# A macaron block on one core: other orders in the opening, at the handover between stages and in the last stage

## The chip, the cores and the metric

The kernel runs on one core of a Trainium2 chip. The metric is the device time of one execution in microseconds, as the median of several runs. The core has five engines with queues of their own: TensorE (PE; matrix products, transposes and weight loads), VectorE (DVE), ScalarE (ACT), GpSimd (POOL) and SyncE (SP), which here only issues transfers. Each works through its instructions strictly in the order in which they are written, and engines wait for each other through semaphores. An instruction that waits holds up everything behind it on its engine.

## The reference

The block takes x of 4 × 1024 tokens with 1024 features and adds three parts to it, one after the other. FFN is a gated linear layer, used twice with the same weights:

```
dots = softmax(LN(x) @ centroids.T / 0.1); hits = dots > 0.01
query_sel = any(hits, axis=1); cluster_sel = any(hits, axis=0)   # over all tokens
out = where(query_sel[:, None] & cluster_sel[assignments], LN(x) @ weight.T + bias, 0)

x = x + 0.5 * FFN(LN(x))
x = x + attention(LN(x))      # each token by itself: 32 heads attend to 32 heads, 8 kv heads repeated 4 times
x = x + 0.5 * FFN(LN(x))
```

`cluster_sel` needs the hits of all tokens, so no output of a FFN is final before the last token has been through its softmax.

## The kernel before, in words

The 4096 tokens are 32 tiles of 128. A matrix product is made of three matmuls for each of 8 blocks of 128 features (k-groups): operands are split into a high and a low part, and high·high, high·low and low·high are summed (`product`, which also takes a table `between` of work to put ahead of a k-group). A product of a tile has two halves of 512 columns, written (t, h) here. To split a tile, ScalarE copies the turned tile to the high part (`high_...`), VectorE subtracts to get the low part (`low_...`), and TensorE needs both.

**Stage one** (`product_first`) makes the first FFN. In the opening the weight rows come in eight loads and are turned by TensorE in 16 blocks of 4 transposes (`transpose_rows`), each into one of five banks by the table `W_BANK`; a block waits until the low part of the block that had the bank before (`low_rows`) is made. Block j covers rows of group j // 2 and half the features. Tiles 0 to 3 are turned by TensorE. From tile 4 on a normed tile is stored to memory (`store_normed`), loaded back in 32-token blocks by four loads (`load_blocks`), and turned within blocks by VectorE (`turn_first`). Tiles go in pairs: `pair_first` makes the softmax logits of two tiles, ScalarE copies them (`copy_pair`), `fold_pair` transposes them, VectorE and ScalarE make the softmax. VectorE evicts each half with the bias (`read_first`), GpSimd masks it by token (`select_tokens`), SP stores it to `f1_d` (`store_first`). All transfers of the stage stand in the one SP queue, in an order that is written by hand.

**The handover.** When the last pair is through its softmax, `select_count` and `select_rows` give the column mask on TensorE, ScalarE copies it (`select_mask`), GpSimd masks tile 0 of `f1_d` and adds x (`mask_first`, `add_first`), VectorE takes statistics, GpSimd the factors, ScalarE the norm, and TensorE transposes. **Stage two** runs over i, with several tiles in flight: products of the last tiles of stage one, q, k and v, scores, heads, and products of the second FFN. q and k of a tile go to memory and back in head order (`qkv_d`); scores wait for that.

**The last stage** runs over 14 late tiles (`LATE`, number v): `transpose_late`, `high_late`, `low_late`, two half products, and `read_late` and `add_late`, beside `finish_ready` for tiles whose product is already made. `store_late` stores a late tile.

TensorE's transposes of late tile v + 1 wait for `low_late(v)`:

```
                def transpose_late(v):
                    pe.wait_ge(yl, v)
                    ...
                        pe.wait_ge(lol, v - 1)
                    transposes(pe, late_y[v % 2]).then_inc(tl, 1)
```

## Time and profile before

| | before |
|---|---|
| median of 3 runs | 1248.04 us (1247.98 to 1249.10) |
| profiled execution, its own time | 1247.12 us |
| its span, first to last instruction | 1245.3 us |
| TensorE busy | 1214.8 us, 98% |
| VectorE busy | 855.7 us, 69% |
| ScalarE busy | 412.6 us, 33% |
| GpSimd busy | 422.6 us, 34% |
| mean granted TensorE clock | 0.993 |

Times in the trace are us from the start of the span. Where a row ends in brackets, the number is how long the engine stood idle before it, and behind the arrow is what released it. `PEclk` is the granted clock of TensorE as a share of full (2.4 GHz). The chain that ended last consists of TensorE for 87% of the span.

### The profile page before, as it was taken

The page shows a single profiled execution, that of the slowest core. Times are in us where ns is not written, and L with a number is a line of the kernel's source. Part 1 is how long each engine was busy: PE and PEld are TensorE (multiplying, and loading weights), DVE is VectorE, ACT ScalarE, POOL GpSimd, SP SyncE. Part 2 cuts the span into 40 slices and gives each one's busy share as a digit, 9 for nine tenths or more (in the row PEclk, how much of TensorE's full clock was granted, in tenths as well). Part 3 has the DMA queues.
Part 4 walks back from the last instruction along what each step waited for, and adds up shares of the span by engine and source line. Part 5 has one row for each costly group of instructions (what it writes and reads, how often), then busy time and mean ns, then how long its engine had stood idle before and what let it go on. Part 6 is the DMA issues. An engine that isn't in the chain of part 4 may idle for free.

```text
span 1245.3 us, 21665 instructions
## 1 busy us (share of the span) xinstructions
PE 1214.8 (98%) x8488; PEld 1042.0 (84%) x8488; DVE 855.7 (69%) x1270; ACT 412.6 (33%) x590; POOL 422.6 (34%) x551
## 2 busy tenths in 40 slices
PE   6999999999997999999999999999999999999998
PEld 5778888888886788888888888888888888887886
DVE  5654465456453377888888888888888875289787
ACT  4222223222220234444444444444444443212120
POOL 1225454543423634323333333333332200040332
PEclk9999999999999899999999999999999999999999
DMA  7376776786663345555555555555565555116875
GB/s 262 102 211 191 238 208 187 189 231 190 161 181 123 106 118 159 157 140 161 154 142 152 152 154 162 135 163 137 153 163 145 142 144 171 51 57 238 293 283 194
DMA packets 318694, 208.54 MB, mean 167 GB/s; under 512 B 258304, under 2 KB 281344, under 8 KB 318592
## 3 DMA queue, kind: packets, MB, share of 16 engines
q1 hardware_dynamic: 303712, 187.74, 53.1%
q10 hardware_dynamic: 14880, 19.40, 4.5%
q8 instruction: 68, 1.11, 0.4%
q14 instruction: 34, 0.28, 0.1%
HBM read 118.49 MB, written 88.60 MB: 166 GB/s over the span
## 4 chain that ended last, share of the span: by engine, by line
PE 87%; DVE 4%; DMA 4%; ACT 2%; SPq 1%; issue 1%; POOL 1%; POOLq 0%; DVEq 0%; ACTq 0%
PE ps_b L268 13%; PE ps_b L270 13%; PE ps_b L269 13%; PE ps_a L268 10%; PE ps_a L270 10%; PE ps_a L269 10%; PE ps_t L275 6%; PE ps_s L1351 5%; PE ps_s L282 2%; PE ps_s L284 2%; DMA y_scratch<-xa 2%; PE ps_s L1401 2%; SPq L402 1%; DMA ya_tok<-y_scratch 1%; DVE ya_tok L939 1%
## 5 line engine op out<-in xcount | busy, mean ns | idle before, releaser
L268 PE MATMUL ps_a<-w_hi,odd_hi 128*128 128x512 f32 x464 | 187.0, 403 | 0.0
L270 PE MATMUL ps_a<-w_hi,odd_lo 128*128 128x512 f32 x464 | 182.4, 393 | 0.0
L269 PE MATMUL ps_a<-w_lo,odd_hi 128*128 128x512 f32 x464 | 182.0, 392 | 0.0
L268 PE MATMUL ps_b<-proj_hi,y_hi 128*128 128x256 f32 (+1 forms) x512 | 177.7, 347 | 0.0
L270 PE MATMUL ps_b<-proj_hi,y_lo 128*128 128x256 f32 (+1 forms) x512 | 172.7, 337 | 0.0
L269 PE MATMUL ps_b<-proj_lo,y_hi 128*128 128x256 f32 (+1 forms) x512 | 172.0, 336 | 0.0
L301 POOL TENSOR_TENSOR var_eps<-moments,eps 128x1 f32<-128x1 f32 x96 | 18.2, 190 | 412.8 <-DVE moments L297 412.8
L665 POOL TENSOR_TENSOR x_ring<-x_ring,f_tmp 128x1024 f32<-128x1024 f32 x32 | 77.0, 2407 | 151.0 <-DVE probs L1115 117.3
L966 DVE TENSOR_TENSOR f_out<-ps_b,bias_a 128x512 f32<-128x512 f32 x30 | 20.7, 689 | 143.6 <-PE ps_b L270 143.6
L611 POOL TENSOR_SCALAR f_out<-f_out,token_on 128x1024 f32<-128x1024 f32 x30 | 85.6, 2854 | 83.2 <-DVE f_out L966 82.9
L270 PEld LDWEIGHTS ps_b<-proj_hi,y_lo 128*128 128x128 f32 x512 | 97.1, 190 | 10.8
L269 PEld LDWEIGHTS ps_b<-proj_lo,y_hi 128*128 128x128 f32 x512 | 97.3, 190 | 9.4
L268 PEld LDWEIGHTS ps_b<-proj_hi,y_hi 128*128 128x128 f32 x512 | 97.2, 190 | 9.0
L270 PEld LDWEIGHTS ps_a<-w_hi,odd_lo 128*128 128x128 f32 x464 | 87.8, 189 | 19.0
L268 PEld LDWEIGHTS ps_a<-w_hi,odd_hi 128*128 128x128 f32 x464 | 88.1, 190 | 17.6
L269 PEld LDWEIGHTS ps_a<-w_lo,odd_hi 128*128 128x128 f32 x464 | 88.2, 190 | 17.2
L310 ACT ACTIVATE q_diag<-x_ring,norms 128x1024 f32<-128x1024 f32 x64 | 79.6, 1244 | 62.2 <-PE ps_s L1351 40.4
L704 POOL TENSOR_TENSOR late<-late,mask 128x1024 f32<-128x1024 f32 x18 | 46.0, 2569 | 137.9 <-DMA late<-x_scratch 91.2
L1073 DVE TENSOR_TENSOR y_lo<-ps_t,y_hi 128x1024 fp32r<-128x1024 f32 x32 | 39.2, 1225 | 65.7 <-ACT y_hi L851 65.7
L268 PE MATMUL ps_b<-w_hi,odd_hi 128*128 128x512 f32 x208 | 81.7, 393 | 0.0
L270 PE MATMUL ps_b<-w_hi,odd_lo 128*128 128x512 f32 x208 | 81.2, 390 | 0.0
L269 PE MATMUL ps_b<-w_lo,odd_hi 128*128 128x512 f32 x208 | 81.1, 390 | 0.0
(189 smaller groups left out, 2722.5 us busy)
## 6 DMA issues: line engine op xcount, KB each, us to landing
xa<-in_L_attn_x SPq DMA_DIRECT2D x32, 512.0 KB, 5.1
f_tmp<-f_scratch SPq DMA_DIRECT2D x32, 512.0 KB, 4.6
x_ring<-in_L_attn_x SPq DMA_DIRECT2D x32, 512.0 KB, 3.3
f_scratch<-f_out SPq DMA_DIRECT2D x30, 512.0 KB, 3.8
x_scratch<-x_ring SPq DMA_DIRECT2D x30, 512.0 KB, 3.3
y_scratch<-xa SPq DMA_DIRECT2D x28, 512.0 KB, 4.5
ya_tok<-y_scratch SPq DMA_DIRECT2D x112, 128.0 KB, 3.3
late<-x_scratch SPq DMA_DIRECT2D x22, 512.0 KB, 7.2
```

Source lines behind the costliest of these rows:

```text
L268: pe.matmul(acc, hi[:, k, :], w_h[:, k, cols], start=(k == 0), stop=False)
L269: pe.matmul(acc, hi[:, k, :], w_l[:, k, cols], start=False, stop=False)
L270: last = pe.matmul(acc, lo[:, k, :], w_h[:, k, cols], start=False, stop=(k == KB - 1))
L275: last = pe.transpose(ps_t[:, k, :], src[:, k * P:(k + 1) * P], ident[:, :])
L282: last = pe.matmul(pair_ps, cen[:, k, :], hi[:, k, :, :], start=(k == 0), stop=(k == KB - 1))
L284: pe.matmul(pair_ps[0:NCL, :], cen[:, k, 0:NCL], lo[:, k, :, :], start=False, stop=False)
L310: return act.activation(y, x, ACT.Identity, bias=norms[of][:, t, 0:1], scale=norms[of][:, t, 1:2])
L611: pool.tensor_scalar(f_out[t % 2][:, :], f_out[t % 2][:, :], token_on[0][:, t:t + 1], None, ALU.mult).then_inc(f1_on, 1)
L665: pool.tensor_tensor(x_ring[t % RING][:, :], x_ring[t % RING][:, :], f_tmp[:, :], ALU.add).then_inc(x1, 1)
L704: pool.tensor_tensor(f[:, :], f[:, :], mask[:, :], ALU.mult).then_inc(s_masked, 1)
L1073: dve.tensor_tensor(y2_lo[:, :, :], ps_t[:, :, :], y2_hi[:, :, :].bitcast(F32), ALU.subtract).then_inc(lo2, 1)
L1351: last = pe.matmul(ps_s[:, j * P:(j + 1) * P], q_diag[:, j * P:(j + 1) * P], k_blocks[:, j, :, :], start=True, stop=True)
```

## The change

It makes no other arithmetic, apart from two half products that are made in two parts of 256 columns.

- Opening: the first half product (0,0) is made by `product_opening` in two parts, the first of which needs blocks 0 to 3 only; blocks go to other banks; norms, low parts and statistics stand in another order on ScalarE and VectorE.
- Tiles 4 and 5: statistics, factors and norm stand earlier; `fold_pair` and `pair_first(2)` stand later on TensorE.
- Tile 31: loaded earlier, stored directly behind tile 30 on a semaphore of its own, its low part ahead of an eviction, and the logits of its pair behind the half product instead of inside it.
- Handover: the loads for stage two (`load_attention`) stand ahead of the store of tile 28; the first transposes of stage two stand inside product (29,1); VectorE evicts (29,1) behind the first statistics.
- Last stage: `low_late(4)` one tile earlier; the last half product, its eviction and its store in two parts.

```diff
-        W_BANK = [0, 1, 2, 3, 0, 1, 2, 3, 1, 3, 4, 1, 3, 4, 1, 3]
+        W_BANK = [0, 1, 2, 3, 4, 1, 2, 3, 4, 1, 3, 4, 1, 3, 4, 1]
...
+        def late_parts(v, h):
+            if v == NL - 1 and h == 1:
+                return [slice(HALF, HALF + QUARTER), slice(HALF + QUARTER, EMB)]
+            return [half(h)]
...
                 def load_blocks(t):
-                    sp.wait_ge(y_stored, 16 * (t + 1 - BY_PE))
+                    if t == LAST:
+                        sp.wait_ge(y_last_stored, 32)
+                    else:
+                        sp.wait_ge(y_stored, 16 * (t + 1 - BY_PE))
...
+                def load_attention():
+                    sp.wait_ge(lo1, NT)
+                    sp.wait_ge(f1_stored[0], 16)
+                    sp.dma_start(f_tmp[:, :], f1_d[0]).then_inc(f_in, 16)
+                    for t in range(RING - 1):
+                        sp.dma_start(x_ring[t % RING][:, :], x_d[t]).then_inc(x_in[t % RING], 16)
...
-                    if 2 * p + 5 < NT:
+                    if 2 * p + 5 < LAST:
                         load_first(2 * p + 5)
                     if 2 * p + 4 < NT:
                         store_normed(2 * p + 4)
+                        if 2 * p + 5 == LAST:
+                            store_normed(LAST)
                         load_blocks(2 * p + 4)
                     if 2 * p + 6 < NT:
                         load_first(2 * p + 6)
+                    if p == NP - 2:
+                        load_attention()
                     store_first(2 * p)
-                    if 2 * p + 5 < NT:
+                    if 2 * p + 5 < LAST:
                         store_normed(2 * p + 5)
+                    if 2 * p + 7 == LAST:
+                        load_first(LAST)
...
@@ -635,11 +653,9 @@
-                    if 2 * p + 5 < NT and p > 0:
+                    if 2 * p + 5 < NT:
                         factors_first(2 * p + 5)
                     select_tokens(2 * p)
-                    if p == 0:
-                        factors_first(2 * p + 5)
...
@@ -746,32 +762,31 @@
                 high_rows(0)
+                norm_first(0)
                 high_rows(1)
-                norm_first(0)
                 high_rows(2)
-                high_rows(3)
                 high_first(0)
-                for j in range(4, 8):
+                for j in range(3, 8):
                     high_rows(j)
...
                     high_first(2 * p + 2)
+                    if p == 0:
+                        norm_first(2 * p + 4)
                     pair_soft_exp(act, p)
                     if p == 0:
-                        norm_first(2 * p + 4)
                         high_first(2 * p + 3)
...
@@ -973,21 +991,21 @@
-                for j in range(4):
+                for j in range(3):
                     low_rows(j)
                 low_first(0)
-                for j in range(4, 8):
+                for j in range(3, 6):
                     low_rows(j)
                 stats_first(1)
...
                 read_first(1, 0)
+                stats_first(4)
                 low_first(2)
                 pair_soft_in(dve, 0)
                 pair_soft_out(dve, 0, 0)
-                stats_first(4)
+                stats_first(5)
                 read_first(0, 1)
                 low_first(3)
-                stats_first(5)
...
                 turn_first(LAST)
+                low_first(LAST)
                 read_first(NT - 5, 1)
-                low_first(LAST)
...
+                    if i == 0:
+                        read_first(NT - 3, 1)
...
-                        if 3 < v + 1 < NL:
+                        if 4 < v + 1 < NL:
                             low_late(v + 1)
                     base_late(v)
+                    if v == 2:
+                        low_late(4)
...
@@ -1225,6 +1252,15 @@
+                def product_opening(between_a, between_b):
+                    hi, lo = first_set(0)
+                    pe.wait_ge(lo1, 1)
+                    pe.wait_ge(wt_lo, 4)
+                    product(pe, ps_a[:, 0:QUARTER], hi, lo, w_hi, w_lo, slice(0, QUARTER), between_a)
+                    pe.wait_ge(wt_lo, 8)
+                    product(pe, ps_a[:, QUARTER:HALF], hi, lo, w_hi, w_lo, slice(QUARTER, HALF),
+                            between_b).then_inc(ffn1[0], 1)
...
                 for p in range(1, NP - 2):
-                    fold_pair(p)
-                    product_first(2 * p, 0)
+                    product_first(2 * p, 0, {3 if p == 1 else 1: lambda: fold_pair(p)})
                     product_first(2 * p, 1)
-                    pair_first(p + 1)
+                    if p > 1:
+                        pair_first(p + 1)
                     product_first(2 * p + 1, 0)
+                    if p == 1:
+                        pair_first(p + 1)
...
-                product_first(NT - 4, 0, {5: lambda: pair_first(NP - 1)})
-                product_first(NT - 4, 1, {2: lambda: fold_pair(NP - 1)})
-                product_first(NT - 3, 0, {1: lambda: select_count(pe, 0), 4: lambda: select_rows(pe, 0)})
-                product_first(NT - 3, 1)
+                product_first(NT - 4, 0)
+                pair_first(NP - 1)
+                product_first(NT - 4, 1, {1: lambda: fold_pair(NP - 1)})
+                product_first(NT - 3, 0, {1: lambda: select_count(pe, 0), 3: lambda: select_rows(pe, 0)})
+                product_first(NT - 3, 1, {6: lambda: transpose_second(0)})
```

TensorE at the start of the program; `w_raw` are the weight rows, `even_hi` and `even_lo` the parts of tile 0, `ya_tok` ahead of the product tile 0 and inside it the centroids. Before:

```order
3 L275 MATMUL ps_t<-ident,ya_tok 128x128 x8
4 L1214 MATMUL ps_a<-ident,w_raw 128x128 x8
5 L1214 MATMUL ps_b<-ident,w_raw 128x128 x8
6 L268 MATMUL ps_a<-w_hi,even_hi 128x512
7 L269 MATMUL ps_a<-w_lo,even_hi 128x512
8 L270 MATMUL ps_a<-w_hi,even_lo 128x512
9 L1244 MATMUL ps_s<-ident,ya_tok 128x64 x8
```

Of the change, the same place:

```order
3 L283 MATMUL ps_t<-ident,ya_tok 128x128 x8
4 L1241 MATMUL ps_s<-ident,w_raw 128x128 x4
5 L1241 MATMUL ps_a<-ident,w_raw 128x128 x4
6 L1241 MATMUL ps_b<-ident,w_raw 128x128 x8
7 L276 MATMUL ps_a<-w_hi,even_hi 128x256
8 L277 MATMUL ps_a<-w_lo,even_hi 128x256
9 L278 MATMUL ps_a<-w_hi,even_lo 128x256
10 L1288 MATMUL ps_s<-ident,ya_tok 128x64 x8
```

The blocks ahead of the product are the same, block 4 in another bank, and the product's matmuls have 256 columns.

SP's queue at the end of stage one, from the store of tile 30 on; `ya_tok<-y_scratch` are the four loads of a tile's blocks, `f_scratch<-f_out` a `store_first`. Before:

```order
143 L391 DMA y_scratch<-xa 128x1024
144 L402 DMA ya_tok<-y_scratch 32x32x32 x4
145 L407 DMA f_scratch<-f_out 128x1024
146 L391 DMA y_scratch<-xa 128x1024
147 L402 DMA ya_tok<-y_scratch 32x32x32 x4
148 L407 DMA f_scratch<-f_out 128x1024 x2
149 L454 DMA f_tmp<-f_scratch 128x1024
150 L456 DMA x_ring<-in_L_attn_x 128x1024 x4
```

Of the change:

```order
143 L399 DMA y_scratch<-xa 128x1024 x2
144 L413 DMA ya_tok<-y_scratch 32x32x32 x4
145 L418 DMA f_scratch<-f_out 128x1024
146 L413 DMA ya_tok<-y_scratch 32x32x32 x4
147 L418 DMA f_scratch<-f_out 128x1024
148 L423 DMA f_tmp<-f_scratch 128x1024
149 L425 DMA x_ring<-in_L_attn_x 128x1024 x4
150 L418 DMA f_scratch<-f_out 128x1024
```

The stores of tiles 30 and 31 now stand together ahead of the loads of tile 30, and the five loads of stage two stand ahead of the last of these stores of `f_out`, that of tile 28.

VectorE in the last stage, from `base_late(2)` on (first row); L1164 and L1166 are the two operations of `finish_ready`, L1146 and L1153 `read_late` and `add_late`, and the `odd_lo` row is `low_late(4)`. Before:

```order
1142 L1140 SCALAR_TENSOR_TENSOR late<-k_diag,token_on,late 128x1024
1143 L1164 SCALAR_TENSOR_TENSOR x_ring<-k_diag,token_on,x_ring 128x1024
1144 L1166 SCALAR_TENSOR_TENSOR x_ring<-late,token_on,x_ring 128x1024
1145 L1164 SCALAR_TENSOR_TENSOR x_ring<-k_diag,token_on,x_ring 128x1024
1146 L1166 SCALAR_TENSOR_TENSOR x_ring<-late,token_on,x_ring 128x1024
1147 L1146 SCALAR_TENSOR_TENSOR v_diag<-ps_a,token_on,mask 128x512
1148 L1153 TENSOR_TENSOR late<-late,v_diag 128x512
1149 L1146 SCALAR_TENSOR_TENSOR v_diag<-ps_a,token_on,mask 128x512
1150 L1153 TENSOR_TENSOR late<-late,v_diag 128x512
1151 L1053 TENSOR_TENSOR odd_lo<-ps_t,odd_hi 128x8x128
```

Of the change:

```order
1145 L1159 SCALAR_TENSOR_TENSOR late<-k_diag,token_on,late 128x1024
1146 L1070 TENSOR_TENSOR odd_lo<-ps_t,odd_hi 128x8x128
1147 L1183 SCALAR_TENSOR_TENSOR x_ring<-k_diag,token_on,x_ring 128x1024
1148 L1185 SCALAR_TENSOR_TENSOR x_ring<-late,token_on,x_ring 128x1024
1149 L1183 SCALAR_TENSOR_TENSOR x_ring<-k_diag,token_on,x_ring 128x1024
1150 L1185 SCALAR_TENSOR_TENSOR x_ring<-late,token_on,x_ring 128x1024
```

The low part has moved ahead of four finishing operations and four of late tile 2.

## Rows read from the trace of the kernel before

**Rows 1.** TensorE's waits, whole span: operation, what released it, us in total, times, longest

```profile
PE ps_s L282 <- DVE odd_lo L944: 4.7, 2, 3.9
...
PE ps_s L282 <- DVE even_lo L944: 2.9, 2, 2.5
PE ps_s L289 <- ACT pair_sums L732: 2.1, 1, 2.1
PE ps_t L275 <- DVE odd_lo L1053: 1.7, 1, 1.7
```

**Rows 2.** Windows, whole trace: busy us of the engines, granted clock, DMA share, GB/s

```profile
core 0: us, PE busy (x) PEld busy (x) DVE busy (x) ACT busy (x) POOL busy (x), PEclk, DMA share, GB/s
...
16.00:20.50 4.50, 4.50 (x20) 3.46 (x20) 1.02 (x3) 1.13 (x3) 1.03 (x4) 0.62 1.02 406
...
54.50:58.50 4.00, 4.00 (x12) 3.23 (x13) 1.50 (x3) 0.25 (x1) 1.21 (x1) 0.57 1.06 259
...
378.50:382.00 3.50, 3.50 (x17) 3.50 (x18) 0.00 (x0) 0.00 (x1) 0.57 (x1) 0.55 0.37 150
...
407.30:413.00 5.70, 5.70 (x18) 4.83 (x19) 1.23 (x1) 1.01 (x1) 5.56 (x3) 0.50 0.24 95
...
431.00:1100.00 669.00, 668.95 (x5890) 587.68 (x5890) 517.01 (x742) 276.49 (x422) 202.12 (x309) 1.00 0.52 143
```

**Rows 3.** Timeline of TensorE in the opening: start, us, what, idle before

```profile
15.77 0.47 PE L268 MATMUL ps_a<-w_hi,even_hi 128*128 128x512 f32 x1 [3.10 <-DVE w_lo L950]
...
70.00 0.38 PE L282 MATMUL ps_s<-even_hi,cen 128*128 128x256 f32 x1 [2.55 <-DVE even_lo L944]
...
94.03 0.28 PE L282 MATMUL ps_s<-odd_hi,cen 128*128 128x256 f32 x1
```

**Rows 4.** Timeline of VectorE in the opening

```profile
13.15 1.28 DVE L950 TENSOR_TENSOR w_lo<-ps_a,w_hi 128x512 fp32r<-128x512 f32 x2
...
66.36 1.25 DVE L939 STREAM_TRANSPOSE ya_tok<-ya_tok 128x1024 f32<-128x1024 f32 x1 [2.99 <-DMA ya_tok<-y_scratch]
```

**Rows 5.** Windows over 24 matmuls of 512 columns, and over 24 of 256

```profile
416.36:421.80 5.44, 5.44 (x25) 4.50 (x24) 0.69 (x1) 1.15 (x1) 4.23 (x3) 1.00 0.13 48
421.80:424.68 2.88, 2.88 (x26) 2.88 (x25) 0.69 (x1) 0.00 (x0) 1.85 (x1) 1.00 0.44 71
```

**Rows 6.** Timeline of SP's queue: a store of a normed tile, loads of tile 7

```profile
48.05 0.33 SPq L391 DMA_DIRECT2D y_scratch<-xa  x1
...
83.08 2.82 SPq L402 DMA_DIRECT2D ya_tok<-y_scratch  x4
```

**Rows 7.** The page's DMA issues: count, KB each, median us from issue to landing

```profile
ya_tok<-y_scratch SPq DMA_DIRECT2D x112, 128.0 KB, 3.3
```

**Rows 8.** Timelines of SP's queue and VectorE at the last pair

```profile
368.47 3.18 SPq L402 DMA_DIRECT2D ya_tok<-y_scratch  x4
...
376.57 1.85 DVE L944 TENSOR_TENSOR odd_lo<-ya_tok,odd_hi 128x1024 fp32r<-128x1024 f32 x1 [0.54 <-ACT odd_hi L722]
```

**Rows 9.** Timelines of ScalarE, GpSimd and TensorE at the handover

```profile
393.80 1.01 ACT L373 CAST mask<-ps_s 128x1024 bf16<-128x1024 f32 x1 [6.35 <-PE ps_s L368]
...
390.84 2.85 POOL L611 TENSOR_SCALAR f_out<-f_out,token_on 128x1024 f32<-128x1024 f32 x1 [11.77 <-DVE f_out L966]
398.53 2.14 POOL L659 TENSOR_TENSOR f_tmp<-f_tmp,mask 128x1024 f32<-128x1024 f32 x1 [4.85 <-DMA f_tmp<-f_scratch]
...
407.28 1.97 PE L275 MATMUL ps_t<-ident,q_diag 128*128 128x128 f32 x8 [5.09 <-ACT q_diag L310]
```

**Rows 10.** Timelines of SP's queue and TensorE: scatter of tile 0, its scores

```profile
422.72 0.37 SPq L521 DMA_DIRECT2D qkv_scratch<-qkv_tok  x1
...
431.23 2.05 PE L1351 MATMUL ps_s<-k_diag,q_diag 128*128 128x128 f32 x16
```

**Rows 11.** Timeline of VectorE: the low part of late tile 4

```profile
1122.20 1.22 DVE L1053 TENSOR_TENSOR odd_lo<-ps_t,odd_hi 128x1024 fp32r<-128x1024 f32 x1
```

**Rows 12.** DMA issues: in the last 10 us, and over the whole span

```profile
out<-late ACTq DMA_DIRECT2D x1, 512.0 KB, 2.6
...
f_scratch<-f_out SPq DMA_DIRECT2D x6, 128.0 KB, 2.4
```

More of the change, by code:

```diff
@@ L1035, in _ @@
                 select_on(dve, 0)
-                for h in range(2):
-                    read_first(NT - 3, h)
+                read_first(NT - 3, 0)
                 GROUPS = "p (c e) -> p c e"
```

79 lines of the change are left out of this document (44 added, 35 removed).

## The prediction

> **What bounds the kernel now.** I read the waits of TensorE first, then the granted clock by stretch, then the order of time around each wait. Through the middle nothing is left to gain by order: from 431 to 1100 us TensorE is busy in 668.95 of 669.00 us, at full clock [rows 2]. The change adds or removes no arithmetic, so only two things can pay: the waits in which TensorE stands still, and the stretches after them in which it works at a lower clock. The reader should see in [rows 1] how few they are (two stand in other groups): in the opening 3.1 us before the first product (for `w_lo` [rows 3]), 0.8 and 2.5 us before pair logits (the singles in the groups `odd_lo` and `even_lo` of L282), 2.1 us before the first fold of pair 1; at the end of stage one 3.9 us before the logits of the last pair; at the handover to stage two 5.1 us for the first normed tile [rows 9]; 1.7 us early in the last stage. Behind four of them the granted clock is 0.62, 0.57, 0.55 and 0.50 of full for 4.5, 4.0, 3.5 and 5.7 us [rows 2], partly the 1.2 GHz level: that loses about 4.5·0.38 = 1.7, 4.0·0.43 = 1.7, 3.5·0.45 = 1.6 and 5.7·0.50 = 2.9 us. Waits and clock together are 19.1 + 7.9 = 27 us. The tail behind the last product is the other part.
>
> **Opening, first product.** Today product (0,0) needs all eight blocks of the first column half and starts at 15.77 [rows 3]. In the new order its first 256 columns need blocks 0 to 3 only. The low part of block 3 now stands behind the low part of tile 0 on VectorE; work in that place starts at 13.15 and takes 0.64 a block [rows 4], so four blocks are ready at 13.8. Block 7 uses the bank of block 3, and its transposes stand ahead of the product, so TensorE waits there until 13.8 and starts the product near 14.25: 1.5 us won of 3.1, and about 1.7 of waiting kept, in a new place. Transposes of blocks 12 and 13 go from product (1,0) into (0,0); the work is the same and I count nothing. Two parts of 256 columns cost more starts: 24 matmuls of 256 columns take 2.88 us, 24 of 512 take 5.44 [rows 5], so a split half costs 5.76 − 5.44 = 0.3 us. The Trainium skill ("TensorE: Matmul & The Clock Gate", section "Wait — 56ns, not 53.3ns?") gives N/2.4 + 2.5 ns from start to start, which would make the split cost 0.06 us; the row decides, since the rows show 120 ns a matmul where that rule has 109.
>
> **Opening, tiles 2 to 5.** Statistics of tiles 4 and 5 now run one place earlier each, their norms on ScalarE ahead of a softmax exponential, and the factors of tile 5 on GpSimd ahead of a masking of 2.85 us (the same operation as tile 28's in [rows 9]). I walked the new order with the durations of the trace. Norm of tile 4 ends near 36.6 and its store is issued then, not at 48.05 [rows 6]. The low part of tile 3 is ready at 43.1 and TensorE asks for it at about 45: the 0.8 goes. The copy of pair 1 no longer stands behind a norm that waits for its factors, and the fold comes three k-groups (2.0 us) into product (2,0): the 2.1 goes. The logits of pair 2 come 5.4 us later in TensorE's order, behind product (3,0), while the turned tile 5 should be there at 57, 9 us earlier than its 66.36 [rows 4]: the 2.5 goes. With 1.5 for the start, 5.4 for these three, 0.3 of a small wait before product (1,0), and 3.4 of clock, less 0.3 for the split, TensorE ends tile 3 some 10.3 us earlier; reckoned with the starts of the timeline it is up to 11.4. I take 10.7.
>
> **What is late next.** Tile 7. Its normed tile goes to memory and back in blocks through the one SP queue. From the turn of tile 5 (66.36 [rows 4]) to the end of the issue of tile 7's four loads (83.08 + 2.82 [rows 6]) are 19.5 us, and a load lands 3.3 us after its issue [rows 7]. With the turn at 57.2 its blocks are there at 79 to 80; turn, high and low part take as long as for tile 5, 66.36 to the end of the wait at 70.0, 3.6 us [rows 3, 4]. So TensorE gets tile 7 at 82.6 to 83.6. It asks at 94.03 − 10.7 = 83.3 [rows 3]. I take 0.5 us of a new wait: **opening −10.2**, bounds −7 and −12.5. Afterwards two tiles take TensorE 24.0 us (70.00 to 94.03 [rows 3]) and this round trip 19.5 + 3.3 = 22.8, so it holds.
>
> **Last pair of stage one.** Tile 31 is stored directly behind tile 30, on a semaphore of its own, so its four loads go out near 365.9 instead of 368.47 [rows 8]. The price: the loads of tile 30 wait in the SP queue behind that store, 1.8 us; the turn of 30, its high and low part and the softmax of pair 14 move by about as much. The low part of tile 31 goes ahead of an eviction (0.65) and so also out of the way of GpSimd's masking, beside which it took 1.85 us [rows 8] where such a low part takes 1.22 by itself [rows 11]; it should end near 376.8, not 378.4. The logits are asked for three k-groups later, at 376.4. The 3.9 shrinks to 0.4 and the clock behind it holds: 3.5 + 1.6 = **−5.1**, bounds −3 and −5.5.
>
> **Handover.** Today the load of `f1` waits in the queue behind the store of tile 28, and x tile 0 is masked at 398.53, though the mask was ready at 394.8 [rows 9]. The new order loads it some 14 us earlier, and the counts come one k-group (0.7) sooner. GpSimd is free of tile 28 at 393.7 [rows 9] and the mask is set at 394.1, so masking starts at 394.1. From masking to TensorE's transposes are 407.28 − 398.53 = 8.75 us [rows 9]; VectorE's eviction of (29,1) now stands behind the statistics, so it doesn't hold them up. The transposes can start at 402.9. They now stand two k-groups before the end of (29,1), so TensorE waits from 400.0: 2.9 instead of 5.1, with 1.4 us of work moved behind it. But the next gate is elsewhere: SP stores half a tile 30 before it may scatter q and k of tile 0. That store waits for GpSimd's masking of tiles 29 and 30, which now waits for the end of (29,1); it goes out at 417.9 if the clock holds and at 419.3 if it falls. The scatter follows 0.3 later. From scatter to scores are 431.23 − 422.72 = 8.5 us [rows 10]. Scores start at 426.4 to 428.0, not 431.23: **−4.0**, bounds −2.5 and −5.
>
> **Last stage and tail.** `low_late(4)` runs at 1122.20 behind three finished tiles' work [rows 11], and the transposes wait 1.7 for it. Moved ahead of two finishing tiles it ends near 1113.7, long before 1121.9: **−1.7**, all of it, since VectorE still reads tile 2 in time. In the tail the last half comes in two parts, each evicted and stored by itself: +0.3 of TensorE, as above. VectorE is nearly full there, so I count 0.3 us won of two operations of half the width. The last store of 512 KB lands after 2.6 us, one of 128 KB elsewhere after 2.4 [rows 12]; with less in flight I take 0.5. **Tail −0.8**, bounds 0 and −1.3.
>
> **Sum.** 10.2 + 5.1 + 4.0 + 1.7 + 0.8 = 21.8 us. The profiled execution takes 1247.12; it becomes 1225.3. The median of before is 1248.04, 0.9 above that execution, so I predict **1226 us**.
>
> **Rivals.**
> *The clock stays low behind the waits that are left.* Those of 1.7 us at 12 and 2.9 us at 400 are as long as some of today's behind which it fell (2.1), and one of 2.5 had no low stretch behind it [rows 1, 2]. If both fall, 1.7 and about 1 us more go, and tile 7's wait grows little, since TensorE comes later. With the lower bounds of the opening it gives 1229 to 1233. The Trainium skill (the same page, section "What's actually happening") says that the default state is throttled and activity releases the throttle. By that rule, the traces agreeing, a short wait alone doesn't tell which it will be.
> *All covers hold.* The clock holds everywhere, tile 7 comes in time and the scores follow at 426: opening 12, last pair 5.5, handover 5, 1.7 and 1.3: 25.5 us, 1222.5.
> *The round trip becomes the bound and the change is slower.* Place: the SP queue, tiles 6 to 29. Without slack every pair waits for its second tile. For it speaks that SP issues all loads and stores of a pair in order and that the slack is only 24.0 − 22.8 = 1.2 us; against it, that the waits of [rows 1] hold no pair logits between 94 and 370 us. Twelve pairs times the overrun must pass 21.8 us, so it decides from 1.8 us a pair (25.8 instead of 24.0). An overrun of 0.5 costs 6 us, 1232; one of 2.5 gives 1256.
> *The early loads do nothing.* If the handover is held by the half tile 30 store alone (its GpSimd chain 3 us longer than I walk it), it gives 1 and the result is 1229.
>
> **How the numbers follow.** The walk as it stands 0.58 (1222.5 to 1229); clock or a small overrun 0.22 (1229 to 1234); all covers 0.13 (1220 to 1222.5); a round trip bound 0.05, half of it slower than before; other 0.02. 1220.5 to 1234 leaves less than 2 in 10 out. Measurements tell 0.2% (2.5 us) from no change; no case ends within it but a thin slice of the overrun. Faster 0.95, same 0.02, slower 0.03.
>
> **What would show it.** Waits of TensorE in the new trace: about 1.7 on a block transpose near 12, none or under 1.5 at tile 7, under 1 at 376, 2 to 3 on the first `q_diag` transposes, and perhaps one on the scores of tile 0; none on `late` transposes. Pair logits of pair 3 begin near 83.5. I am wrong if TensorE waits again and again for `odd_lo` or `even_lo` between 90 and 360 us, if the clock is at half for long in the first 20 us, or if the scores of tile 0, due at 431.2 − 10.2 − 5.1 − 4.0 = 411.9, begin later than 415.

## The result, and the profile after

The changed kernel takes 1228.59 us, median of 4 runs (1227.52 to 1229.05), against 1248.12 (4 runs, 1247.98 to 1249.1): ratio 0.9842, 95% interval 0.9824 to 0.9859, so 1.6% faster. The forecast was 1226, range 1220.5 to 1234. Its profiled execution takes 1228.51 us, span 1226.7; TensorE is busy for 1208.9 us of it.

The waits of TensorE that are left, whole span; they answer to [rows 1]:

```profile
PE ps_a L1241 <- DMA w_raw<-in_L_ffn_weight: 5.8, 1, 5.8
PE ps_s L1400 <- ACT q_diag L883: 3.3, 1, 3.3
PE ps_t L283 <- ACT q_diag L318: 2.3, 1, 2.3
PE ps_b L1241 <- DVE w_lo L968: 1.7, 1, 1.7
PE ps_s L290 <- DVE odd_lo L962: 0.9, 1, 0.9
```

The first line, the wait for the first weights, is in both kernels. Of the other 19.2 us (the seven waits of the kernel before add up to that, not to 19.1), 8.2 are left. Five of the old waits are gone: both at the logits of pairs 1 and 2, the fold, the late transposes, and the 3.1 before the first product. Two are new: 1.7 us before a block of weight transposes, which the prediction had named, and 3.3 us before the scores of tile 0 (L1400).

Windows of 4 us around the two waits of the handover; the column before the last two is the granted clock ([rows 2]):

```profile
384.00:388.00 4.00, 1.72 (x11) 1.18 (x10) 0.87 (x3) 1.24 (x1) 1.04 (x4) 1.00 0.37 131
388.00:392.00 4.00, 4.00 (x21) 3.37 (x20) 1.82 (x2) 1.02 (x1) 1.16 (x1) 1.00 0.00 0
...
412.00:416.00 4.00, 2.64 (x15) 2.64 (x16) 0.00 (x0) 1.31 (x4) 2.08 (x2) 0.75 0.53 161
416.00:420.00 4.00, 4.00 (x17) 3.36 (x17) 3.36 (x3) 0.88 (x1) 0.80 (x1) 0.82 0.22 74
```

The stretch from 412 to 420 is the only one before the tail in which the clock is below full: it held behind 2.3 us of waiting and fell behind 3.3. The loss is 4·(0.25 + 0.18) = 1.7 us. In the kernel before it fell four times.

Timeline of TensorE at the marks that the prediction names (start, us, what, idle before), answering to [rows 3, 9, 10]:

```profile
14.58 0.63 PE L1241 MATMUL ps_b<-ident,w_raw 128*128 128x128 f32 x4 [1.74 <-DVE w_lo L968]
14.96 0.36 PE L276 MATMUL ps_a<-w_hi,even_hi 128*128 128x256 f32 x1
83.62 0.28 PE L290 MATMUL ps_s<-odd_hi,cen 128*128 128x256 f32 x1
366.44 0.38 PE L290 MATMUL ps_s<-odd_hi,cen 128*128 128x256 f32 x1 [0.89 <-DVE odd_lo L962]
387.43 1.09 PE L283 MATMUL ps_t<-ident,q_diag 128*128 128x128 f32 x8 [2.28 <-ACT q_diag L318]
413.36 3.21 PE L1400 MATMUL ps_s<-k_diag,q_diag 128*128 128x128 f32 x16 [3.33 <-ACT q_diag L883]
```

Pair 3 starts 10.4 us earlier than before (94.03). The count (`select_count`, the first matmul of the column mask at the end of stage one) comes 15.6 earlier (374.90 for 390.53), so the last pair gave 5.2. At the scores 17.9 are won, but the 16 matmuls there take 3.21 us, not 2.05: the clock. At the transposes of tile 2, behind that stretch, 16.3 are left of it (425.21 for 441.48), so **the handover, costed at 4.0, gave 0.6 in this trace** (2.5 in a second trace of the same kernel, e9 below). At the count of stage two 15.9 are left (1070.02 for 1085.90); TensorE has no wait in between that accounts for the 0.4. The last stage gives 1.9 more, and the tail 0.8.

Where the new wait comes from: VectorE's copy of q and k, GpSimd, SyncE's queue and ScalarE ahead of the scores:

```profile
400.85 0.69 DVE L1129 TENSOR_TENSOR qkv_tok<-ps_b,proj_bias 128x512 f32<-128x512 f32 x1 [0.28 <-PE ps_b L278]
401.16 1.57 POOL L696 TENSOR_SCALAR f_out<-f_out,token_on 128x512 f32<-128x512 f32 x1
402.76 0.32 SPq L527 DMA_DIRECT2D f_scratch<-f_out  x1
403.12 0.43 SPq L539 DMA_DIRECT2D qkv_scratch<-qkv_tok  x1
407.92 0.65 SPq L543 DMA_DIRECT2D q_head<-qkv_scratch  x1
411.61 1.70 ACT L883 ACTIVATE q_diag<-q_head,own_t 128x256 f32<-128x256 f32 x4 [5.99 <-DMA q_head<-qkv_scratch]
```

The scatter (L539) writes q and k of tile 0 to memory. Its data are ready at 401.54, but the store of the first half of tile 30 (L527, the half store from here on) stands ahead of it in SyncE's queue, and it goes out 1.6 us later, at 403.12. The load of `q_head` (L543) is issued once the scatter has landed. That took 407.92 − 403.12 = 4.8 us; in the kernel before it took 3.0 [rows 10]:

```profile
419.02 0.32 SPq L509 DMA_DIRECT2D f_scratch<-f_out  x1
422.72 0.37 SPq L521 DMA_DIRECT2D qkv_scratch<-qkv_tok  x1
425.71 0.65 SPq L525 DMA_DIRECT2D q_head<-qkv_scratch  x1
```

What differs: before, the half store had gone out 3.7 us ahead of the scatter; now it goes out 0.36 us ahead, and both are under way together. The 1.6 of standing in the queue and the 1.8 of longer landing are the wait of 3.3.

The end of the changed kernel, VectorE:

```profile
1218.76 1.28 DVE L1183 SCALAR_TENSOR_TENSOR late<-k_diag,token_on,late 128x1024 f32<-128x1024 f32 x1 [3.18 <-POOL late L720]
...
1224.04 0.42 DVE L1224 TENSOR_TENSOR late<-late,v_diag 128x256 f32<-128x256 f32 x1
```

From the end of the last matmul to the end of the span are 3.44 us (4.58 before); less 0.3 for the split, 0.8 is won. VectorE starts its last stretch late, on a tile that GpSimd finishes (L720).

### The profile page after: what moved, and what is told of

Its sections match the earlier page's. It is cut to its first block, busy times and chain, and to the rows that moved or that the text cites. A ratio compares the mean times of both kernels' runs of the same rounds, so it can differ in the third digit from the quotient of the medians.

```text
span 1226.7 us, 21763 instructions
## 1 busy us (share of the span) xinstructions
PE 1208.9 (99%) x8536; PEld 1041.3 (85%) x8536; DVE 856.9 (70%) x1272; ACT 413.1 (34%) x590; POOL 420.8 (34%) x551
## 4 chain that ended last, share of the span: by engine, by line
PE 82%; DVE 7%; DMA 4%; issue 3%; POOL 2%; ACT 1%; SPq 1%; POOLq 0%; DVEq 0%; ACTq 0%
PE ps_b L276 12%; PE ps_b L278 12%; PE ps_b L277 12%; PE ps_a L276 9%; PE ps_a L278 9%; PE ps_a L277 9%; PE ps_t L283 5%; PE ps_s L1400 5%; PE ps_s L290 2%; DMA late<-x_scratch 2%; PE ps_s L292 2%; PE ps_s L1445 2%; DVE late L1183 1%; DVE v_diag L1165 1%; POOL late L720 1%
## 5 line engine op out<-in xcount | busy, mean ns | idle before, releaser
L276 PE MATMUL ps_a<-w_hi,odd_hi 128*128 128x512 f32 (+1 forms) x472 | 187.4, 397 | 0.0
L278 PE MATMUL ps_a<-w_hi,odd_lo 128*128 128x512 f32 (+1 forms) x472 | 183.5, 389 | 0.0
L277 PE MATMUL ps_a<-w_lo,odd_hi 128*128 128x512 f32 (+1 forms) x472 | 183.0, 388 | 0.0
L278 PEld LDWEIGHTS ps_a<-w_hi,odd_lo 128*128 128x128 f32 x472 | 88.6, 188 | 18.6
L720 POOL TENSOR_TENSOR late<-late,mask 128x1024 f32<-128x1024 f32 x18 | 43.9, 2450 | 138.5 <-DMA late<-x_scratch 91.7
L276 PE MATMUL ps_b<-w_hi,odd_hi 128*128 128x512 f32 (+1 forms) x208 | 80.8, 389 | 0.0
L278 PE MATMUL ps_b<-w_hi,odd_lo 128*128 128x512 f32 (+1 forms) x208 | 80.3, 386 | 0.0
L277 PE MATMUL ps_b<-w_lo,odd_hi 128*128 128x512 f32 (+1 forms) x208 | 80.3, 386 | 0.0
```

The lines of the kernel that those rows point to most:

```text
L276: pe.matmul(acc, hi[:, k, :], w_h[:, k, cols], start=(k == 0), stop=False)
L277: pe.matmul(acc, hi[:, k, :], w_l[:, k, cols], start=False, stop=False)
L278: last = pe.matmul(acc, lo[:, k, :], w_h[:, k, cols], start=False, stop=(k == KB - 1))
L720: pool.tensor_tensor(f[:, :], f[:, :], mask[:, :], ALU.mult).then_inc(s_masked, 1)
```

## The experiments

Three sets (e1 to e4, e5 to e8, e9 to e12), each beside the kernel before on the same chip (medians there 1250.62, 1249.13 and 1251.17 us). Behind a time stands its spread, lowest to highest; behind a ratio to the kernel before, its 95% interval. "The stretch" is the time from the count to the transposes of tile 2: 50.95 us in the kernel before, 50.31 in the changed kernel.

**Where tile 30's half store stands.** `e1_scatter_first` moves it from ahead of the scatter of q, k and v to behind the loads of tile 0's heads:

```diff
-                    if i == 1:
-                        sp.wait_ge(f1_on, NT - 1)
-                        sp.dma_start(f1_d[NT - 2][:, half(0)], f_out[0][:, half(0)]).then_inc(f1_stored[0], 16)
...
+                    if i == 1:
+                        sp.wait_ge(f1_on, NT - 1)
+                        sp.dma_start(f1_d[NT - 2][:, half(0)], f_out[0][:, half(0)]).then_inc(f1_stored[0], 16)
```

> The changed kernel with one thing moved: SP issues the scatter of q and k of tile 0 (and what follows it for that tile) before the store of the first half of tile 30. In the changed kernel TensorE waited 3.33 us for the scores of tile 0, at 413.36, and worked at a lower clock for about 4 us behind it. Theory A, the queue: the scatter was held 1.6 us behind that store, and landed in 4.8 us instead of 3.0 because the two transfers were in flight together. Then the scatter goes out at 401.6, the scores start at about 410.1 without a wait, and the low stretch behind them is gone too: 3.3 + 1.6 = 4.9 us less, about 1223.7. Theory B, the chain from q's load to its diagonal on ScalarE is itself too long for the earlier TensorE: the wait stays above 2.5 us and the time stays within 1 us of 1228.6.

1228.46 us (1226.49 to 1231.1), ratio 0.9821 (0.98 to 0.9841). SyncE's queue and ScalarE:

```profile
403.17 0.38 SPq L536 DMA_DIRECT2D qkv_scratch<-qkv_tok  x1
406.17 0.65 SPq L540 DMA_DIRECT2D q_head<-qkv_scratch  x1
...
409.89 1.71 ACT L883 ACTIVATE q_diag<-q_head,own_t 128x256 f32<-128x256 f32 x4 [2.68 <-DMA q_head<-qkv_scratch]
```

The scatter goes out as soon as its data are there. That is no earlier than in the changed kernel, because here the clock fell before it and VectorE's copy starts at 402.45, not at 400.85. It lands in 3.0 us, and the scores follow at 411.65 without a wait. So both parts of the wait are gone, the 1.6 behind the store and the 1.8 of longer landing. The median doesn't show it: 1228.46 for 1228.59. In the profiled execution the clock fell behind the unchanged 2.28 us wait at the transposes instead of at the scores:

```profile
387.43 1.51 PE L283 MATMUL ps_t<-ident,q_diag 128*128 128x128 f32 x8 [2.28 <-ACT q_diag L318]
...
388.00:392.00 4.00, 4.00 (x14) 3.32 (x13) 0.46 (x1) 1.01 (x1) 0.00 (x0) 0.58 0.00 0
```

Same start and same wait as in the changed kernel's profile, and another clock: 0.58 for 1.00. The stretch takes 46.99 us, 3.3 less (4.9 expected); the clock fall, which only changed its place, is the difference.

**The handover undone.** `e2_handover_old`: loads of `f1` and x behind the last pair's queue, eviction (29,1) ahead, `select_rows` at k-group 4, and tile 0's transposes behind the whole product.

```diff
-                    if p == NP - 2:
-                        load_attention()
...
-                product_first(NT - 3, 1, {6: lambda: transpose_second(0)})
+                product_first(NT - 3, 1)
```

> The changed kernel with the handover in the orders of before: loads for stage two behind the store of tile 28, first transposes of stage two behind product (29,1), eviction of (29,1) ahead of the first statistics, column mask one k-group later. All else as changed. If the handover's part of the change is worth what I forecast (4.0 us), this gives 1232.6. By the marks in the two traces it is worth 0.6 us (15.63 us ahead at the counts, 16.27 at the transposes of tile 2): theory A says 1229.2, with waits of 5.1 us at the first transposes and none at the scores.

1234.96 us (1231.82 to 1236.07), ratio 0.9865 (0.9844 to 0.9885). The median lies above both numbers, 1229.2 and 1232.6, and decides nothing. The trace has the waits of theory A: one of 5.12 at the transposes, none at the scores. The stretch takes 50.33 us, in the changed kernel 50.31: in these two traces, the handover edits as they stand trade one wait for two. Of the 3.3 us by which its span is longer, 2.6 are there at the count already, from a wait of 2.21 at pair 3 and one of 1.83 instead of 0.89 at the last pair.

**The transposes later.** `e3_transposes_later` puts tile 0's transposes into the next half product; `e4_both` is that with the order of e1.

```diff
-                product_first(NT - 3, 1, {6: lambda: transpose_second(0)})
+                product_first(NT - 3, 1)
...
-                        product_first(LAST - 1 + (i - 1) // 2, (i - 1) % 2)
+                        product_first(LAST - 1 + (i - 1) // 2, (i - 1) % 2,
+                                      {2: lambda: transpose_second(0)} if i == 1 else {})
```

> The changed kernel with the first transposes of stage two not in product (29,1) but two k-groups into product (30,0), 1.4 + 1.4 us of work later, so that TensorE doesn't stand 2.28 us for the normed tile, and (29,1) ends and is evicted 3 us earlier. Order of SP as in the changed kernel. Theory A: the wait of 2.28 goes; the half-tile store goes out near 399.0 and the scatter right behind it at 399.4, still sharing the way, so the scores start near 409.6 behind a wait of about 2 us: 3.7 us less, near 1225, or 1226 if the clock falls further. Theory B: the wait moves to the scores in full (over 4.5 us) and nothing is won.

1225.88 us (1225.48 to 1226.35), ratio 0.9796 (0.9779 to 0.9814). No wait at the transposes, 0.9 at the scores, clock at full: the stretch takes 43.79 us, 6.5 less. That is more than the 3.7 expected, for two reasons: the low clock went too, and the scatter, again 0.37 us behind the half store, landed in 3.4 us here (403.28 to 406.66), not in 4.8.

> Both edits: scatter ahead of the half-tile store, first transposes two k-groups into (30,0). Theory A: no wait at the transposes, none or under 1 us at the scores, which start near 407.6, and no low stretch: 5.8 + 1.6 = 7.4 us less than the changed kernel, near 1221.2. Theory B: as the changed kernel, 1228.

1226.21 us (1221.77 to 1227.34), ratio 0.9792 (0.9769 to 0.9816). The stretch takes 43.02, 7.3 less, as expected. The median didn't follow as far (1221.2 expected), nor did e3's by all of its 6.5: both profiles show a wait for tile 7 at pair 3 (1.87 and 2.07 us) that the changed kernel's profile has not, with a clock fall behind it.

**The second tile of pair 2.** `e5_store5_first`:

```diff
+                    if p == 0:
+                        store_normed(5)
                     store_first(2 * p)
-                    if 2 * p + 5 < LAST:
+                    if 0 < p and 2 * p + 5 < LAST:
                         store_normed(2 * p + 5)
```

> The changed kernel; SyncE stores normed tile 5 one place earlier, ahead of the first store of pair 0. Theory (the late store of the next normed tile is what opens the wait at the third pair, 0 to 2.2 us long from one execution to the next): the chain of tile 5 and with it that of tile 7 moves 1.5 to 2 us earlier, the wait at the transposes of tile 7 is gone, the logits of pair 3 start at 83.1 to 83.7 us. Rival (the wait is the speed of the chip's DMA in that execution, not the place of the store): the logits of pair 3 stay anywhere between 83.6 and 85.5 us and the median is that of the changed kernel, 1228.6. By the theory 1226.5 to 1228.6, by how often the changed kernel waits there.

1232.81 us (1227.98 to 1235.76), ratio 0.9862 (0.9841 to 0.9883). The profile shows what the theory says (no wait, pair 3 at 82.83), yet the median is above all that was expected (1226.5 to 1228.6), and no trace shows why: the profiled execution is the fastest of the five. One profile can't tell how often the wait comes, and the two waits of the handover are still there. Inconclusive by itself.

**The opening, and the last stage, undone.** `e6_opening_old` puts back every order of the opening and the whole first product (W_BANK among them), `e7_late_tail_old` these:

```diff
-            if v == NL - 1 and h == 1:
-                return [slice(HALF, HALF + QUARTER), slice(HALF + QUARTER, EMB)]
...
-                        if 4 < v + 1 < NL:
+                        if 3 < v + 1 < NL:
                             low_late(v + 1)
...
-                    if v == 2:
-                        low_late(4)
```

> The changed kernel with all orders of the opening as they were before (turns, first rows, first product whole, fold and pair order of pair 1); the last pair, the handover and the last stage stay as changed. Theory (the terms add): the opening's 10.4 us come back, the count starts at 385.3 us and the median is 1238.5 to 1239.5. Rival (what the opening gained is in part taken back by later stages, since transfers of stage one start earlier against the same traffic): under 9 us come back, 1237 or less.

1240.9 us (1237.6 to 1242.93), ratio 0.9934 (0.9918 to 0.995), 11 to 12 us above the changed kernel, more than the theory's 1238.5 to 1239.5. In its trace the count comes at 387.92, 13.0 later: the 10.4, and besides a wait for tile 5's low part of 3.85 where the kernel before had 2.55, with a clock fall that there was not there. No later stage took anything back; the rival falls.

> The changed kernel with two edits of the last stage undone: VectorE's low rows of late tile 4 at their old place, and the last late tile's second half stored in one part. Theory: the wait of 1.7 us at the transposes of late tile 4 is back (1.9 with the clock behind it) and the tail is 0.8 longer, 1231.3. Rival for the tail (the store was not the end, the chain through the last finishing tile is): the tail stays as long as it is, 1230.5.

1234.87 us (1230.47 to 1239.43), ratio 0.9885 (0.9864 to 0.9907): its executions lie 9 us apart, too far for 2.7 us. The trace is plain. The wait is back at its old place, and from the end of the last matmul to the end of the span are 4.34 us, not 3.44:

```profile
1108.42 1.06 PE L281 MATMUL ps_t<-ident,f_tmp 128*128 128x128 f32 x8 [1.70 <-DVE odd_lo L1068]
...
1225.17 0.39 PE L276 MATMUL ps_b<-w_hi,odd_lo 128*128 128x512 f32 x1
...
1226.75 0.69 DVE L1220 TENSOR_TENSOR late<-late,v_diag 128x512 f32<-128x512 f32 x1
```

From the count of stage two to the end it takes 2.5 us more than the changed kernel (159.14 for 156.68): 1.9 ahead of the tail, and 0.9 less the 0.3 of the split in it.

**All orders that the runs pointed to.** `e8_all`: e1, e3 and e5 together, the transposes of block 7 inside the first product, and the last late tile's first half read ahead of the last finishing tile. `e11_three_orders`, in the third set, is e1, e3 and e5 alone.

> The changed kernel with the orders that the runs so far point to: the half store of tile 30 behind the scatter of keys and queries, the transposes of tile 0's queries later (in the second of the four half products instead of the first), the store of normed tile 5 ahead of the first store of pair 0, the transposes of block 7 inside the first product's first columns, and the last late tile's first half read and added ahead of the last finishing tile. Theory: the handover gives 7.3 us, the opening 0.45, the tail 0.4, no wait at pair 3: 1220.4. Rivals: the earlier product only finds later rows of weights late and waits there instead (opening 0, 1221); moving the read ahead of the finishing tile lengthens the tail by that read, since the chain through the finishing tile is the last (0.4 slower, 1221.2); with both, 1221.6.

1220.71 us (1220.18 to 1222.56), ratio 0.9779 (0.9765 to 0.9793). The stretch takes 42.79 us. The two small orders: the tail is 3.2 us instead of 3.5 of e11 (0.3 won). The first product now waits its 1.7 us itself (start 13.95), and the count comes at 374.67, for 374.90 in the changed kernel and 373.69 in e11: nothing shows that the earlier product brought anything.

> The run with all orders less its two small ones: half store of tile 30 behind the scatter, transposes of tile 0's queries later, store of normed tile 5 first. Theory: 7.4 us of the handover, 1221.2 to 1221.7, and executions close together (within 3 us), since TensorE has no wait of 2 us left. Rival (the two small orders carried more, or the store of tile 5 does nothing): 1224 and more, or a wait at pair 3 in the profile.

1222.76 us (1220.68 to 1224.94), ratio 0.9782 (0.9763 to 0.9801). Its profiled execution is the fastest; in two of the others the mean clock was 0.998 and 0.999, which points to a clock fall that no profile shows. All that TensorE waits for in the profile, whole span:

```profile
PE ps_a L1243 <- DMA w_raw<-in_L_ffn_weight: 5.9, 1, 5.9
PE ps_b L1243 <- DVE w_lo L970: 1.7, 1, 1.7
PE ps_s L290 <- DVE odd_lo L964: 0.9, 1, 0.9
PE ps_s L1403 <- issue: 0.2, 1, 0.2
PE ps_s L1403 <- ACT q_diag L885: 0.2, 1, 0.2
```

**The changed kernel again**, in the third set, unedited:

> The changed kernel itself, run again beside the next three. By the first two sets its variants spread over 4 to 9 us from one execution to the next where they keep waits of 2 us and more on TensorE, and over 2.4 us where they keep none. Theory (each such wait may or may not have a stretch of low clock behind it, worth 1.7 us, and the wait at the third pair is 0 to 2.2 us long): executions between 1227 and 1236, median 1229 to 1232, and the profile may show the wait at pair 3, or none, and clock below 1.00 behind the transposes of tile 0's queries, or not. Rival (it repeats as the first measurement did): all within 1227.5 to 1229.1.

1229.54 us (1227.98 to 1234.09), ratio 0.9835 (0.9815 to 0.9856); the intervals of e8 and e11 lie wholly below it. Its own profile has what the first had not, a wait at pair 3, and a clock fall behind the transposes instead of the scores. The scatter landed in 3.4 us (406.40 to 409.78), not in 4.8, so the wait at the scores is 1.4, and the stretch takes 48.43 us, 2.5 less than in the kernel before. The scores start at 415.04, just past the 415 that the prediction had named as a sign of being wrong:

```profile
85.23 0.38 PE L290 MATMUL ps_s<-odd_hi,cen 128*128 128x256 f32 x1 [1.73 <-DVE odd_lo L962]
...
389.40 1.25 PE L283 MATMUL ps_t<-ident,q_diag 128*128 128x128 f32 x8 [2.29 <-ACT q_diag L318]
415.04 1.16 PE L1400 MATMUL ps_s<-k_diag,q_diag 128*128 128x128 f32 x8 [1.44 <-ACT q_diag L883]
...
388.00:392.00 4.00, 2.60 (x12) 2.31 (x13) 0.00 (x0) 2.25 (x2) 0.07 (x1) 0.78 0.02 8
392.00:396.00 4.00, 4.00 (x15) 3.19 (x15) 1.82 (x2) 0.00 (x0) 1.87 (x1) 0.80 0.00 0
```

Why pair 3 waits here and not there: SyncE's queue stores normed tile 6 (L399) and loads its blocks (L413) once the store has landed; tile 7's come behind. First the changed kernel's first profile, then this one's:

```profile
60.53 0.32 SPq L399 DMA_DIRECT2D y_scratch<-xa  x1
63.40 3.02 SPq L413 DMA_DIRECT2D ya_tok<-y_scratch  x4
```

```profile
60.75 0.32 SPq L399 DMA_DIRECT2D y_scratch<-xa  x1
65.24 3.12 SPq L413 DMA_DIRECT2D ya_tok<-y_scratch  x4
```

Issued within 0.2 us of each other, the loads follow after 2.9 us in one execution and 4.5 in the other (4.6 and 5.1 in e3 and e4, which waited too; 2.6 and 3.2 in e5 and e11, which didn't). The Trainium skill ("DMA: Bandwidth & Descriptors", section "Latency and other measured facts") says that the latency of the memory is the larger part of a transfer's fixed cost and grows with its load. These rows show a range of 2.6 to 5.1 us for one store in one place, but not load as its reason: between 60.5 and 63.4 us the DMA share is 0.47 in the first profile and 0.46 in this one. What made the store late stays open.

**The last pair's orders alone.** `e10_last_pair_orders_old` keeps the early store and loads of tile 31, and puts the low part, the logits and the two folds back:

```diff
+                read_first(NT - 5, 1)
                 low_first(LAST)
-                read_first(NT - 5, 1)
...
-                product_first(NT - 5, 1, {1: lambda: fold_pair(NP - 2)})
-                product_first(NT - 4, 0)
-                pair_first(NP - 1)
-                product_first(NT - 4, 1, {1: lambda: fold_pair(NP - 1)})
+                fold_pair(NP - 2)
+                product_first(NT - 5, 1)
+                product_first(NT - 4, 0, {5: lambda: pair_first(NP - 1)})
+                product_first(NT - 4, 1, {2: lambda: fold_pair(NP - 1)})
```

> The changed kernel with the orders of TensorE and VectorE around the last pair of stage one as before (folds, place of the pair logits in the product, eviction ahead of the low part of tile 31); SyncE's queue stays as changed, so tile 31 is still stored and loaded early. Theory (the 5.2 us came from the logits being asked for three k-groups later and the low part standing first): the wait at the logits of pair 15 grows from 0.9 to 4 us or more, the clock falls behind it, and 4 to 6 us come back: 1233 to 1235. Rival (the earlier store and loads of tile 31 bring it): the wait stays under 1.5 us and 1 us or less comes back: 1229.5.

1233.38 us (1231.33 to 1241.87), ratio 0.9869 (0.9844 to 0.9894). TensorE and VectorE:

```profile
365.59 0.38 PE L290 MATMUL ps_s<-odd_hi,cen 128*128 128x256 f32 x1 [2.02 <-DVE odd_lo L962]
...
363.70 1.83 DVE L962 TENSOR_TENSOR odd_lo<-ya_tok,odd_hi 128x1024 fp32r<-128x1024 f32 x1 [0.55 <-ACT odd_hi L738]
```

Between both: the wait is 2.02, not 4, and from pair 3 to the count are 292.9 us (296.5 before, 291.3 changed). So of the 5.2 us, 3.6 came with the early store and loads (a wait shortened from 3.9 to 2.0, and no clock fall behind it), and 1.6 with the orders. That the clock held behind 2.0 is partly chance, as the last section shows; had it fallen, 1.7 more would be the orders'. The low part behind the eviction takes 1.83 us; ahead of it 1.23 in the changed kernel.

**The first product whole.** `e12_whole_product`:

```diff
-                product_opening({1: transpose_centroids, 4: lambda: transpose_rows(8), 6: lambda: transpose_rows(9)},
...
+                product_first(0, 0, {1: transpose_centroids, 2: lambda: transpose_rows(8),
```

> The changed kernel with the first half product whole again (512 columns at a time, all eight blocks of its weights needed), blocks 8 to 13 transposed inside it; everything else as changed. Theory (the split lets the product start after four blocks): it starts at 15.5 to 16.5 us instead of 14.96 behind a wait near 3 us, gets 0.3 us back from fewer matmuls, and as in the kernel before the clock falls behind the wait, 1.7 us: 1.5 to 3 us slower, 1230 to 1231.6. Rival (the wait only moves, since the low parts come at the same pace, and the clock holds): within 0.5 us of the changed kernel.

1235.38 us (1230.27 to 1235.99), ratio 0.9868 (0.9847 to 0.9889):

```profile
14.62 0.63 PE L1241 MATMUL ps_b<-ident,w_raw 128*128 128x128 f32 x4 [1.43 <-DVE w_lo L968]
18.41 0.47 PE L276 MATMUL ps_a<-w_hi,even_hi 128*128 128x512 f32 x1 [3.15 <-DVE w_lo L968]
```

Both theories miss. The product starts at 18.41, 3.4 us late, and pair 3 at 90.09, 6.5 late; the clock between 16 and 28 us is 0.86, 0.50 and 0.78 in windows of 4 us, which is the other 3.4. VectorE's new order has the statistics of tile 1 ahead of the low parts of blocks 6 and 7, which a split product can bear and a whole one can't: the two edits are a package, and undoing one alone costs more than the start of the product gave with both (0.8, and 1.7 of clock).

## Why the prediction held, and where it didn't

**Opening, −10.2: 10.4.** The 1.7 on the transposes of block 7 is there (1.74); the product starts at 14.96, not 14.25, since VectorE's low part of block 3 started at 13.75 instead of 13.15. That is no fixed number: in the ten traces with these orders and the split product those transposes start anywhere from 13.17 to 14.96. Against the 0.7 stand the 0.5 of a wait for tile 7 that this execution didn't have, so that the sum hit so closely is in part luck. The three waits for tiles 3 and 5 and for the fold are gone, and in this execution the clock holds to 412. Tile 7 was the right next thing, but its price is not the 0.5 that I took: of the eight traces with the opening and its stores as changed, four have no such wait (changed, e1, e7, e10) and four have one of 1.7 to 2.2 us (e9, e3, e4, e2), behind two of which the clock fell. In e3, e4 and e9 the store of tile 6 landed late; in e2 it went out late (62.04 for 60.53), which no run explains. E6 confirms the term by undoing it.

**Last pair, −5.1: 5.2.** The low part of tile 31 ends at 366.4; forecast, less the opening, 366.6. E10 divides it: most came from the earlier store and loads, not from the place of the logits.

**Handover, −4.0: 0.6. This is the step that failed.** Its own bounds were −2.5 and −5. The loads for stage two did their part: TensorE's first transposes wait 2.28 us, and 2.9 were forecast. The queue was right too: the half store was due at 417.9 less 15.3 = 402.6 with the scatter 0.3 behind, and they stand at 402.76 and 403.12. Then the prediction took "from scatter to scores 8.5 us" from a row in which the scatter travelled alone. With the half store beside it, it was 10.2, as 1.8 us went into the landing. So the scores started 1.5 us later than the 411.9 that were due, behind a wait of 3.3, and behind that the clock fell, 1.7, which the sum had at nothing.

The other traces show both terms, and that both vary. The scatter landed in 2.99 to 3.00 us in all six in which the half store isn't just ahead of it (before, e1, e2, e4, e8, e11). With the store 0.36 to 0.37 us ahead it landed in 4.6 to 4.8 in four (changed, e5, e7, e10) and in 3.4 in four (e3, e6, e9, e12). So the neighbour costs 0.4 or 1.6 to 1.8 us, and no run shows what decides which. With 3.4, the changed kernel's handover gave 2.5 us (e9), the lower bound, with a clock fall as well.

E3 and e4 show the second edit that the change had half done: transposes asked two k-groups before the end of (29,1) still wait 2.3; asked in the next half product, they wait for nothing.

The stretch adds up in every trace. Clock losses are 4 us windows times what the clock lacks of 1.00; where TensorE stood still in part of a window only the rest is counted (2.3 of e2, 2.9 of before). "Landing" is from the issue of the scatter to that of the load behind it:

| kernel | landing | stretch | waits | clock | rest |
|---|---|---|---|---|---|
| before | 3.0 | 50.95 | 5.09 | 2.9 | 43.0 |
| changed | 4.8 | 50.31 | 2.28 + 3.33 | 1.7 | 43.0 |
| changed again (e9) | 3.4 | 48.43 | 2.29 + 1.44 | 1.7 | 43.0 |
| e1, store behind | 3.0 | 46.99 | 2.28 | 1.7 | 43.0 |
| e2, handover old | 3.0 | 50.33 | 5.12 | 2.3 | 42.9 |
| e3, transposes later | 3.4 | 43.79 | 0.92 | 0 | 42.9 |
| e5 | 4.8 | 50.42 | 2.28 + 3.44 | 1.7 | 43.0 |
| e6 | 3.4 | 50.60 | 2.28 + 1.99 | 3.4 | 42.9 |
| e7 | 4.6 | 50.09 | 2.28 + 3.10 | 1.7 | 43.0 |
| e10 | 4.8 | 51.58 | 2.29 + 3.00 | 3.4 | 42.9 |
| e12 | 3.4 | 50.45 | 2.27 + 1.86 | 3.4 | 42.9 |
| e4, e8, e11 | 3.0 | 43.02, 42.79, 43.04 | 0 (0.2 in e11) | 0 | 42.8 to 43.0 |

The work is 43 us in all; the rest is waits and the clock behind them. Of the 8 us above it in the kernel before, the change took 0.6 in one trace and 2.5 in another, and e11, with three orders more, has nearly none of them left.

**Last stage and tail, −1.7 and −0.8: 1.9 and 0.8**, by the marks, and 2.5 together in e7's trace. The prediction's own terms for the tail, 0.3 and 0.5 won and 0.3 paid for the split, add up to 0.5; its sum left the 0.3 out. The tail became 1.1 us shorter, 0.8 with the split paid.

**The sum.** 21.8 us were forecast. The terms by the marks add up to 18.9, and the profiled spans differ by 18.6. The handover fell 3.4 short of its price, and the others together gave 0.5 more than theirs. The time stayed inside the range since the range was wide enough for one term to fail.

**The rivals.** The first, a clock that falls behind the waits that are left, is what happened, though not where it was put: at the scores in one execution, at the transposes in others. The second (all covers hold) is e11, with three orders more. The round trip never became the bound: between 94 and 360 us no trace has a wait for a tile above 0.32 us. The fourth (the early loads do nothing, since the half store alone holds the handover: 1 us won, 1229) comes closest to what was measured, 0.6 and 1228.59. But its reason is only half right. The loads brought the first transposes from 16.75 us behind the count to 12.53; it was the scatter, behind and beside the half store, that took most of it back.

## What to carry to other kernels

A latency read from one row holds for the traffic of that row: when a move puts two transfers next to each other on a queue, ask which of them the critical engine waits for, and let that one go first. Cost a wait of two microseconds on TensorE at its own length plus the chance of a clock fall. When an order is changed as a package, undoing one part tells what it is worth inside the package, not by itself.

## What the runs showed of the hardware

**The clock behind waits.** In the 14 traces TensorE waits 11 times for 3.0 us or longer after its first work; the granted clock fell behind all 11. It waits 18 times for 1.8 to 2.6 us; it fell behind 11 and held behind 7, and of the eight waits of 2.27 to 2.29 us at the first transposes of stage two behind five. Behind none of those of 1.74 us and less did it fall. A single fall costs 1.7 us each time (1.68 to 1.72 by the windows), as long as TensorE has work in it; behind three of the waits above 3 us (407 in the kernel before, 394 in e2, 18 in e12) the clock lacks twice as much. So between 1.8 and 2.6 us the length of the wait alone doesn't decide it.

**The spread goes with it only in part.** The changed kernel ran from 1227.5 to 1234.1 in nine executions, and its variants with such waits spread over up to 10.5 us (e10); e8, with no wait over 1.74 us behind the first, over 2.4, at a mean clock of 1.000 in all five. But the first four executions of the changed kernel lie within 1.5 us, and those of e3, with a wait of 1.87 in its trace, within 0.9; and e1 took 1226.69 and 1228.46 at a mean clock of 1.000. So the clock isn't all that varies.

**What isn't settled.** Whether the wait at pair 3 is gone for good with the store of tile 5 first: the three profiles with that order (e5, e8, e11) have none, against four of eight without it, but only one execution of each was traced, and e5's others ran up to 7.8 us longer than it. And what share of the scatter's longer landing is its neighbour's packets and what the completion, no run separates.
